# A decoder block on one Trainium2 core: the opening's second half of the projections, a read-back of columns and the later loads are placed anew

## The reference, cut to what matters

```
x = x + attention(layernorm(x))         # 4 x 1024 x 256, 16 heads of 16, softmax(q k' / 4 + alibi bias) v, then out_w
x = x + cross_attention(layernorm(x))   # one head of 256 over 77 context rows per batch
x = x + moe(layernorm(x))               # 8 experts 256 -> 1024 -> 256, top 2 of a router

qkv = x @ qkv_w.T + qkv_b
scores = einsum('bhid,bhjd->bhij', q, k) / scale + alibi_bias      # -|i-j| * 0.5**head
out = einsum('bhij,bhjd->bhid', softmax(scores), v)
```

## Time and profile before

| | |
|---|---|
| median of 3 runs | 1692.68 us |
| the profiled execution's own time | 1696.51 us |
| its span, first to last instruction | 1694.7 us |
| PE busy | 1617.0 us, 95% |
| DVE busy | 1024.3 us, 60% |
| mean granted TensorE clock | 0.982 of full speed |
| first `score` of group 0 | 110.78 us after the span's start |

### The profile page before, as it was taken

How to read it: one execution, slowest core, us unless ns; L and a number is a source line. 1 busy time by engine, 2 the same in 40 slices (tenths; PEclk the granted TensorE clock), 3 DMA queues, 4 the chain that set the end, 5 groups by cost and what they waited for, 6 DMA issues and landing times.

```text
span 1694.7 us, 29721 instructions
## 1 busy us (share of the span) xinstructions
PE 1617.0 (95%) x10022; PEld 968.4 (57%) x10022; DVE 1024.3 (60%) x2366; ACT 787.6 (46%) x1635; POOL 322.1 (19%) x310
## 2 busy tenths in 40 slices
PE   4889999999999999999999999989999999999997
PEld 2433343344454444444434453369998898999996
DVE  3688877888778778787788775333444232323332
ACT  2137666667646666655676657742221121212211
POOL 5301120001200041210031100332252121221221
PEclk9789999999999999999999999999999999999998
DMA  6930430333241440332431622335566665566662
GB/s 171 177 72 26 78 51 30 42 41 54 52 63 42 76 77 8 41 71 72 66 62 32 140 73 79 111 109 162 155 190 191 180 180 164 175 170 187 171 188 62
DMA packets 92661, 173.30 MB, mean 102 GB/s; under 512 B 13236, under 2 KB 51124, under 8 KB 92385
## 3 DMA queue, kind: packets, MB, share of 16 engines
q1 hardware_dynamic: 75376, 143.69, 33.9%
q0 software_dynamic: 15744, 26.54, 7.4%
q10 hardware_dynamic: 1392, 1.18, 0.3%
HBM read 133.69 MB, written 37.29 MB: 101 GB/s over the span
## 4 chain that ended last, share of the span: by engine, by line
PE 86%; DMA 5%; DVE 3%; ACT 3%; issue 2%; POOL 1%; SPq 0%; ACTq 0%; DVEq 0%; POOLq 0%
PE ps L1028 15%; PE ps L1054 14%; PE ps L1243 13%; PE ps L1014 13%; PE ps L1220 12%; DMA out<-yo,xi 3%; PE ps L1084 3%; DVE rmax L1392 2%; ACT prob L1255 2%; PE ps L1093 2%; PE ps L1106 2%; PE ps L1140 2%; PE ps L1075 2%; PE ps L1057 2%; PE ps L1017 2%
## 5 line engine op out<-in xcount | busy, mean ns | idle before, releaser
L1392 DVE TENSOR_REDUCE rmax<-ps 128x1 f32<-128x512 f32 x1024 | 664.7, 685 | 200.3 <-PE ps L1057 102.7
L1255 ACT ACTIVATE prob<-ps 128x512 f32<-128x512 f32 x1024 | 561.6, 600 | 336.3 <-PE ps L1017 184.3
L1054 PE MATMUL ps<-stacked_k,stacked_q 112*128 112x512 bf16 x1024 | 395.2, 390 | 15.7 <-DMA stacked_k<-parts_of_rows 7.4
L1014 PE MATMUL ps<-stacked_q,stacked_k 115*128 115x512 bf16 x1024 | 360.7, 383 | 7.3 <-ACT prob L1255 5.1
L1028 PE MATMUL ps<-prob,values 128*32 128x512 f32 x2048 | 274.0, 607 | 6.0 <-ACT prob L1255 5.5
L1243 PE MATMUL ps<-w,hidT 128*128 x1136 | 261.4, 384 | 8.1 <-issue 7.9
L1054 PEld LDWEIGHTS ps<-stacked_k,stacked_q 112*128 112x128 bf16 x1024 | 100.3, 98 | 292.3 <-DVE rmax L1392 207.6
L1220 PEld LDWEIGHTS ps<-xiT,w_now 128*128 128x128 f32 x2272 | 265.3, 192 | 3.5
L1220 PE MATMUL ps<-xiT,w_now 128*128 128x128 f32 x2272 | 267.1, 275 | 0.0
L1361 ACT ACTIVATE hidT<-ps,b 128x128 f32<-128x128 f32 x284 | 81.3, 369 | 356.2 <-PE ps L1220 356.2
L1243 PEld LDWEIGHTS ps<-w,hidT 128*128 128x128 f32 x1136 | 211.4, 191 | 40.7 <-issue 14.3
(11 more groups left out here) (181 smaller groups left out, 1134.3 us busy)
## 6 DMA issues: line engine op xcount, KB each, us to landing
w_now<-in_w SPq DMA_DIRECT2D x71, 1024.0 KB, 5.4
stacked_q<-parts_of_rows SPq DMA_DIRECT2D x90, 128.0 KB, 6.5
stacked_k<-parts_of_rows SPq DMA_DIRECT2D x90, 128.0 KB, 7.1
xi<-expert_rows SPq DMA_DIRECT2D x71, 130.0 KB, 2.1
w<-in_w SPq DMA_DIRECT2D x8, 1024.0 KB, 9.7
parts_of_rows<-q_part SPq DMA_DIRECT2D x21, 256.0 KB, 7.9
parts_of_rows<-k_part SPq DMA_DIRECT2D x21, 256.0 KB, 7.7
xr<-in_x POOLq DMA_DIRECT2D x4, 1024.0 KB, 9.7
```

The costliest lines, as they stand in the source:

```text
L1014: m = e.matmul(ps[:, bank, :], ka[i][0:ROWS, hh, kt * P:(kt + 1) * P], qa[i][0:ROWS, hh, ch * BANK:(ch + 1) * BANK], start=True, stop=True)
L1054: m = e.matmul(ps[:, bank, :], qa[i][0:MAX_ROW, hh, qt * P:(qt + 1) * P], ka[i][0:MAX_ROW, hh, kc * BANK:(kc + 1) * BANK], start=True, sto ...
L1255: e.activation(prob[:, u % NPROB, :], ps[:, u % NSCORE, :], ACT.Exp).then_inc(sem["exp"], 1)
L1392: e.tensor_reduce(rmax[:, G % 2, hh * NT + qt, kc:kc + 1], ps[:, p.bank("max", *k), :], AX.X, ALU.max).then_inc(sem["maxed"], 1)
```

## The change

Five things move in the opening; nothing is computed otherwise.

1. The first maxima of group 0 are held back in the plan (`rows_in`) until the planner's clock reaches the landing of their columns, so all four projections of `mo = 1` and the first `vproj` come before the first maximum in every list.
2. ACT's read-back of the second half of k's columns becomes a step of its own (`first_reload`), put behind the two `high` of q of `mo = 1`; before, it stood right behind the copies that it waits for.
3. `context_in` comes on POOL behind `mid` and `low` of the four projections of `mo = 1`, and so does the next batch's load.
4. `fetch_next` and `late_in` come when group 0's `nrow` is planned; `route_setup` comes at the start of group 1; the next batch's preparation starts 10 planned us later than it would.
5. `context_products` start from the 40th maximum (`FIRST_ALONE`), not from the 32nd.

```diff
+FIRST_ALONE = 5 * UNITS // 8
@@ next_batches
-            while now["ended"] < NG * (b - 1):
+            while now["ended"] < NG * (b - 1) or p.pe < landed + 10.0:
@@ plan
     while not split:
         next(opening)
-    add("context_in")
-    add("fetch_next", 1)
-    add("late_in")
...
+    rows_in = [p.emptied["low", 0, 0, 1, 0] + 8.0, p.emptied["low", 0, 0, 1, 1] + 11.0]
     while beside or context or p.pe < landed:
-
-        if context and now["maxima"] >= UNITS // 2:
+        if ("high", 0, 1, 0, 1) in p.number and ("first_reload",) not in p.number:
+            add("first_reload")
+        if ("low", 0, 1, 1, 1) in p.number and ("context_in",) not in p.number:
+
+            add("context_in")
+        if context and now["maxima"] >= FIRST_ALONE:
             beside.append(context.pop())
-        while bank_free() and now["maxima"] < UNITS + LEAD and now["spread"] > now["maxima"] // UNITS:
+        while (bank_free() and now["maxima"] < UNITS + LEAD and now["spread"] > now["maxima"] // UNITS
+               and p.pe >= rows_in[now["maxima"] >= UNITS // 4]):
...
                 landed = p.made["nrow"] + 4.0
-                add("route_setup")
+
+                add("fetch_next", 1)
+                add("late_in")
...
     for G in range(NB * NG):
+        if G == 1:
+            add("route_setup")
@@ scalar
+            def first_keys(ch):
+                cols = slice(ch * BANK, (ch + 1) * BANK)
+                e.wait_ge(sem["first_k"], 16 * NPART * (ch + 1))
+                for j, (_, of_k) in enumerate(PAIRS):
+                    e.dma_start(ka[0][DH * j:DH * (j + 1), :, cols], by_row(stage[0, 1, of_k, 0:HG * DH, cols])).then_inc(sem[("first_rows", "spread0")[ch]], 16)
...
                 elif kind == "first_half":
                     ch, = k
...
                         e.wait_ge(sem["k_ones"], 1)
-                    e.wait_ge(sem["first_k"], 16 * NPART * (ch + 1))
-                    for j, (_, of_k) in enumerate(PAIRS):
-                        e.dma_start(ka[0][DH * j:DH * (j + 1), :, cols], by_row(stage[0, 1, of_k, 0:HG * DH, cols])).then_inc(sem[("first_rows", "spread0")[ch]], 16)
+                        first_keys(0)
+                elif kind == "first_reload":
+                    first_keys(1)
```

More of the change, by code:

```diff
@@ L1292, in _ @@
                     ch, = k
-                    cols = slice(ch * BANK, (ch + 1) * BANK)
                     if ch:
+                        cols = slice(ch * BANK, (ch + 1) * BANK)
                         for n, part in enumerate(("high", "mid", "low")):
```

## The result

| | before | the change |
|---|---|---|
| median of 22 runs each | 1692.76 us | 1687.25 us |
| lowest and highest of them | 1687.62 to 1698.37 | 1682.05 to 1694.79 |
| ratio of the two, 95% interval | | 0.997 [0.9961, 0.9979] |
| the profiled execution's time (span) | 1696.51 (1694.7) us | 1687.17 (1685.3) us |
| mean granted clock | 0.982 | 0.986 |

The change makes the kernel 5.5 us faster (3.6 to 6.6 by the interval). 1684.7 us were forecast, with 1681.5 to 1689.5 as the range: the sign and the mechanism of the opening were right, and the gain was forecast 2.5 us too large.

A forecast was written before the change was run, and what follows sets the result against it. TensorE (PE) was taken to bound the attention groups, with 1 to 2% left over. First score at 102.7, not 110.78 us, gives 8.1, rounded to 8.0: 1692.68 - 8.0 = 1684.7 us, range 1681.5 to 1689.5.

The forecast's parts named there:

- the clock rival: PE at the low clock from 34.9 us: eighth projection 2.0 us more, value projection 1.8 more; 1688.4 us, chance 0.17.
- the second rival: The gain does not arrive: something behind the opening sets the pace, or the stall stays; 1692.7 us, chance 0.09.
- The chain through the stall: Opening: columns landed, POOL's DMAs, `mid`/`low`, `rest`, value projection; PE stood still 5.27 us, `rest` waited 6.41 us for POOL.
- The first maximum: Opening of group 0: starts at about 42.5 us behind eight projections and a value projection, 7 us later than before.
- The maxima alone: Ahead of the context: 33 maxima alone, not 16; 24 at 0.677 us each, 40 reduced at 72.4 us.
- The context to `nmax`: From first context product at 71.5 us, bound by PE with 19 maxima, 23.7 us to `nmax` at 95.2.
- The landing of the row maxima: Between `nmax` and first score: copies issued last at 99.3 us land 3.4 us later, at 102.7, setting the first score.
- The landing rival: Row maxima land behind `fetch` and `fetch_next`: 18.3 us, first score 117.6, 1699.5 us; sign decided from 11.5 us; chance 0.06.
- The opening as a whole: Up to group 0's first score: 102.7 us, not 110.78, a gain of 8.1 us.
- The next batch's preparation slips by about 15 units and still ends ahead of group 3: Groups behind the opening: the later preparation is still ready in time, and group 4's maxima stand at the same place.
- its leftover 1 to 2% in these stretches may change by a us either way: PE in the attention groups: its work is only shuffled, and its idle share may change by a us.
- Moved at no cost, with 1.6 us of cover: ACT's read-back starts at 36.32 us anyway, when its copies have landed; without cover the second half lands up to 1.4 later.

The follow-up runs named there:

- e1: The kernel before, with only POOL's `context_in` DMAs and the next batch's load moved behind `mid` and `low` of `mo = 1`; 1686.67 us, ratio 0.9969.
- e6: The changed kernel with context products begun at the 25th maximum, one behind every third maximum instead of every second; 1691.16 us, ratio 0.9993.
- e9: The changed kernel without the 10 us delay of the next batch's preparation, and with `fetch_next` directly behind `context_in`; 1687.18 us, ratio 0.9971.
- e11: The changed kernel with only the 10 us delay of the next batch's preparation taken out; 1685.44 us, ratio 0.9952.
- e12: The changed kernel run once more with nothing altered; 1687.02 us, ratio 0.9975.
- e3: The changed kernel with the context products started from the 32nd maximum again; 1689.1 us, ratio 0.9986.
- e5: The changed kernel with the later loads, `route_setup` and the next batch's preparation as in the kernel before; 1686.21 us, ratio 0.9962.
- e2: The changed kernel without the holding back of the first maxima (`rows_in` set to 0.0); 1685.4 us, ratio 0.997.
- e4: The changed kernel with ACT's read-back of the second half's key columns back directly behind its copies; 1692.74 us, ratio 1.0005.
- e8: The changed kernel with the hold 4 us shorter, so four maxima lie beside the seventh and eighth projection; 1684.65 us, ratio 0.9959.
- e7: As e6, but from the 27th maximum and with four maxima in the gaps beside the seventh and eighth projection; 1687.59 us, ratio 0.9967.
- e10: e9 with four maxima beside the seventh and eighth projection, as in e8; 1682.71 us, ratio 0.9928 to the kernel before.

## Why the prediction was right, and what it mis-sized

- **The number** is in the stated range by its width. 1687.25 us is 0.25 above the forecast's own range (1682.8 to 1687) and nearer to the clock rival's 1688.4, though not for that rival's reason. By the prediction's own sign (a first score at 103 with the end less than 6 us earlier) the second rival holds in part: 2.2 us of the opening's gain don't arrive.
- **The chain through the stall** was right. e1 removes POOL's DMAs from it and nothing else, and the 6.41 us go.
- **The first maximum**: forecast 42.5, measured 43.21 us, of which 1.0 is the later fourth `rest`. The seventh and eighth projection were to take 3.8 and 1.8 us; the pair took 3.70, at the higher clock for nearly all of it. ACT's and DVE's chain set the value projection's start, so little of that was won. The clock rival's first step did not happen here, and that is luck: with the same eight records behind much the same wait, they took 3.70 us in the change, e6, e9, e11 and e12, but 5.40 in e3 and 6.53 in e5.
- **The maxima alone**: forecast 0.677 us each, measured 22.16/32 = 0.693. The windows of the change show the clock there, against the earlier trace rows:

```profile
57.00:73.60 16.60, 14.43 (x26) 2.63 (x25) 16.11 (x25) 0.00 (x0) 0.00 (x0) 0.50 0.89 200
73.60:97.00 23.40, 22.18 (x96) 11.99 (x94) 16.54 (x27) 5.71 (x13) 1.79 (x2) 0.89 0.61 74
```

  It is at its low level (0.50) from 57.00 us to the first context product; ahead of that PE's maxima last 0.39 us up to 54.4 us, and 0.61 from 55.6. The first context product came at 73.63, not 71.5: 1.4 us since the run starts at 52.40, not 51.0 (1.0 of it the later fourth `rest`), 0.5 by the slower pace.
- **The context to `nmax`**: forecast 23.7, measured 23.3 us.
- **The landing of the row maxima**: forecast 102.7 less 95.2, that is 7.5 us from `nmax` to `score`; measured 7.13. The landing came last, as in the sum: in the change the weight load of the first `score` waits 0.64 us for it (PE's weight loads, and the DMA issues of 80 to 112 us with KB and us to landing).

```profile
104.06 0.10 PEld L1025 LDWEIGHTS ps<-stacked_q,stacked_k 115*128 115x128 bf16 x1 [0.64 <-DMA stacked_q<-nparts_of]
```

```profile
xr_next<-in_x POOLq DMA_DIRECT2D x1, 1024.0 KB, 8.7
```

  The landing rival (11.5 us) is refuted in its size: 3.4 us in e11. Its mechanism isn't. `xr_next` landed at 94.63 + 8.7 = 103.3 us and the `score` started 0.7 us later. In all seven executions that issue the row maxima while `xr_next` is in flight (the change, e2, e4, e6, e8, e11, e12) the `score` or its weight load waits for them, and it starts 0.6 to 0.9 us behind the load's landing, though 2.4 to 4.1 us behind the end of their own issue; `nmax` to `score` is 7.02 to 8.76 us, not 6.78. e9 and e11 differ in the place of this load alone, and have 6.78 and 7.58 us. So the next batch's load, put here by the change, costs 0.2 to 2.0 us (0.35 in the change, 0.9 in e12, 2.0 in e6). The Trainium skill, page "DMA: Bandwidth & Descriptors", section "Queues, rings and completion order", has the DMA engines take turns between queues; no row here shows the three copies landing ahead of the load.
- **The opening as a whole**: 8.1 us forecast; 6.7 measured by the clock, 7.7 from the fourth `rest`.
- **The step that was mis-sized** is "The next batch's preparation slips by about 15 units and still ends ahead of group 3" and, with it, "its leftover 1 to 2% in these stretches may change by a us either way". I asked only whether the preparation is still ready in time. Without it group 0 becomes 1.4 us shorter (64.34 to 62.91), while group 2, which takes it up, becomes 4.0 us longer (57.72 to 61.72) and group 1 0.65. That costs 3.0 us in this stretch, not 1 (1.6 of it PE's idle time, so the preparation also filled PE's gaps; the rest is longer busy time). By the end of group 13 it is 3.7 us: of the 7.7 us, 4.7 are left at group 3 and 4.0 at group 13, and the runs' 5.5 (3.6 to 6.6) agree with that within their scatter.
- **"Moved at no cost, with 1.6 us of cover"** was true for the read-back but undersold: it is the part that makes the hold harmless (e4, 6.5 us).

What stays open: why group 0 alone is shorter (61.3 to 62.1 us) in e3, e6 and e7, which have the delay and another start of the context, so that their second stretch (238.2 to 238.9 us) lies between the two groups; why the same instructions keep PE busy longer when the preparation is moved; and how much of e10's median is owed to six runs only.

## What to carry to other kernels

Look at what is queued behind an instruction that waits: nine DMA issues ahead of eight small operations on one engine, and six ahead of two on another, were worth 5.8 and 6.5 us (the second only beside the hold; the two don't add up), and neither engine was busy. Background work isn't free to move beside an engine that is 98% busy: taking it out of one group gave 1.4 us, putting it into another cost 4.0. A large load put just ahead of a short copy that the critical path waits for has a price too: here the copy never landed before it. Before moving such work, read the busy time of that engine in both places, and ask what would fill the gaps it leaves.

## What the runs showed of the hardware

The same 16 f32 records at the start of the projections end up to 3 us apart in executions of identical code (fourth `rest` at 26.73 us in e5, 29.88 in the change). PE begins them 0.6 us apart (18.19 and 18.79), and 24 records then take 11.33 us in e5 and 13.87 in the change: in e5 a record lasts 592 to 697 ns from the start, in the change 1061 to 1220 ns if it begins before 24 us, and 592 to 697 behind that. The profile's granted clock reads 1.00 from 18.8 to 28 us in both, so here only the records' lengths tell. An opening must be measured from an anchor behind it.

The clock also fell where PE was never idle. The windows of e9 in group 7:

```profile
555.00:565.00 10.00, 10.00 (x67) 6.01 (x66) 5.84 (x13) 2.96 (x6) 0.00 (x0) 0.78 0.88 130
565.00:575.00 10.00, 10.00 (x57) 3.26 (x54) 7.46 (x24) 6.52 (x13) 0.00 (x0) 0.87 0.00 0
```

and of e11 at the same place of the program:

```profile
559.00:569.00 10.00, 10.00 (x78) 5.88 (x74) 6.73 (x17) 3.93 (x8) 0.00 (x0) 1.00 0.83 118
```

PE's records fill 10.00 of 10.00 us in both, and the granted clock is 0.78 and 0.87 in the one, 1.00 in the other. Both have the same row of 128x8 `logits` matmuls there; what made the clock fall isn't shown. The drop cost 3.0 to 3.2 us in e3, e7, e9 and e10 and 1.6 in e1 and e6 (group 7 lasts 56.9 us without it, 59.9 in e9, 58.4 in e1), and nothing in the other eight, the change and e11 among them: as much as one whole part of this change, and with no edit that it goes with. The Trainium skill, page "TensorE: Matmul & The Clock Gate", section "What's actually happening", has the clock depend on activity; here it fell while PE's records filled the stretch.
